# A graph layer's row gathers: 127 partitions on GpSimd, the last partition by SyncE

## The reference

```
h    = max(layernorm(x), 0)                       # 12500 x 64
h0   = attr @ W0 + b0                             # per edge, 32 -> 64
t    = gelu(gelu(h0) @ W1 + b1) @ W2 + b2
score = (h0 + t) @ W3 + b3                        # 412500 x 64
msg  = h[src] * score                             # the gather that the change touches
wV   = segment_sum(msg, dst) / max(count(dst), 1) # 12500 x 64
out  = x + wV @ Wo + bo
```

## Time and profile before

| | |
|---|---|
| median of 3 runs | 4044.81 us |
| span of the profiled execution, first to last instruction | 4042.3 us |
| TensorE busy | 81% of the span |
| GpSimd busy | 75% |
| VectorE, ScalarE busy | 27%, 14% |
| mean granted TensorE clock | 0.785 of full speed |
| mean traffic | 43 GB/s |

### The profile page before, as it was taken

The page is one execution under the profiler, slowest core; times in us unless marked ns, Lnnn a source line. Parts: engine busy times, 40 slices in busy tenths (PEclk is TensorE's granted clock), DMA queues, the critical chain, the costliest instruction groups (busy, mean ns, idle before and its releaser), DMA issues.

```text
span 4042.3 us, 34777 instructions
## 1 busy us (share of the span) xinstructions
PE 3264.8 (81%) x12308; PEld 2146.4 (53%) x12309; DVE 1084.3 (27%) x2563; ACT 585.2 (14%) x838; POOL 3045.3 (75%) x3228
## 2 busy tenths in 40 slices
PE   4988888888888878888888788888887788888879
PEld 2655555555555555555555555555555555555557
DVE  7322222222222222222222222222222222222234
ACT  4211111111111111111111111111111111111111
POOL 7777777777777777777777777777777777777776
PEclk8977777777777777777777777777777777777778
DMA  5211111111111111111111111111111111111112
GB/s 145 48 40 40 40 40 40 40 40 40 40 40 42 40 40 40 40 40 40 40 40 40 40 40 40 40 40 40 41 41 41 40 40 40 40 40 40 40 37 60
DMA packets 217372, 174.70 MB, mean 43 GB/s; under 512 B 112108, under 2 KB 163821, under 8 KB 216920
## 3 DMA queue, kind: packets, MB, share of 16 engines
q0 software_dynamic: 103136, 105.82, 12.1%
q1 hardware_dynamic: 113536, 64.91, 6.0%
q10 hardware_dynamic: 616, 3.20, 0.2%
HBM read 167.28 MB, written 6.40 MB: 43 GB/s over the span
## 4 chain that ended last, share of the span: by engine, by line
POOL 73%; issue 24%; PE 2%; DVE 0%; DMA 0%; POOLq 0%; ACT 0%; DVEq 0%
POOL rows L332 73%; PE ps_h1a L539 0%; PE ps_h1b L539 0%; PE ps_h0a L463 0%; POOLq L353 0%; PE ps_h1b L471 0%; PE ps_h1a L471 0%; PE ps_sb L482 0%; PE ps_sb L477 0%; PE ps_wa L497 0%; PE ps_h0b L463 0%; DMA rows<-h_rows,idx 0%; PE ps_sb L486 0%; PE ps_sa L482 0%; PE ps_sa L477 0%
## 5 line engine op out<-in xcount | busy, mean ns | idle before, releaser
L332 POOL DMA_INDIRECT rows<-h_rows,idx x3175 | 2999.5, 945 | 967.6 <-issue 966.9
L497 PE MATMUL ps_wa<-ln_sq,msg 128*128 128x128 f32 x1616 | 350.1, 385 | 665.6 <-DVE msg L690 665.5
L497 PEld LDWEIGHTS ps_wa<-ln_sq,msg 128*128 128x128 f32 x1616 | 299.2, 276 | 741.2 <-issue 728.1
L690 DVE TENSOR_TENSOR msg<-ps_sa,rows 128x512 f32<-128x512 f32 x202 | 139.7, 691 | 1403.3 <-DMA rows<-h_rows,idx 1391.0
L690 DVE TENSOR_TENSOR msg<-ps_sb,rows 128x512 f32<-128x512 f32 x201 | 139.0, 692 | 1396.8 <-DMA rows<-h_rows,idx 1382.0
L396 ACT ACTIVATE g<-ps_h1a,wp 128x512 f32<-128x512 f32 x202 | 139.0, 688 | 2383.5 <-PE ps_h1a L471 2383.5
L482 PE MATMUL ps_sa<-w_attr,attr 128*128 128x256 f32 x808 | 405.0, 654 | 0.0
L482 PEld LDWEIGHTS ps_sa<-w_attr,attr 128*128 128x128 f32 x808 | 229.8, 314 | 327.0 <-issue 292.6
L477 PE MATMUL ps_sa<-b_last,wp 1*128 1x512 f32 x404 | 403.1, 1097 | 0.0
L486 PEld LDWEIGHTS ps_sa<-w_gelu,g 128*128 128x128 f32 x1616 | 377.5, 321 | 34.3
L486 PE MATMUL ps_sa<-w_gelu,g 128*128 128x128 f32 x1616 | 367.7, 405 | 0.0
(11 more groups left out here) (94 smaller groups left out, 2381.4 us busy)
## 6 DMA issues: line engine op xcount, KB each, us to landing
attr<-in_edges SPq DMA_DIRECT2D x402, 128.0 KB, 3.0
rows<-h_rows,idx POOLq DMA_INDIRECT x3175, 2.4
xs<-in_x SPq DMA_DIRECT2D x4, 700.0 KB
h_rows<-ln_d ACTq DMA_DIRECT2D x4, 700.0 KB
dst_i<-in_dst SPq DMA_DIRECT2D x1, 1612.0 KB, 27.2
idx<-in_src SPq DMA_DIRECT2D x50, 32.0 KB, 2.3
rows<-in_dst_rows SPq DMA_DIRECT2D x4, 384.0 KB
out<-ln_d SPq DMA_DIRECT2D x1, 1530.0 KB
```

Of the source, the lines that this page charges most:

```text
L332: pool.indirect_dma_start(rows[:, slot, t, :], None, table, bass.IndirectOffsetOnAxis(ap=idx[:, part, at, t:t + 1], axis=0),).then_inc(gat ...
L497: pe.matmul(window[0:m * D, 0:m * WIN], msg[:, s % 2, t:t + m, :].rearrange("p t d -> p (t d)"), hot[:, k, t:t + m, :].rearrange("p t n -> ...
L690: dve.tensor_tensor(msg[:, s % 2, 0:n, :], ps_s[s % 2][:, 0:n * D].rearrange("p (t d) -> p t d", d=D), rows[:, s % G_RING, 0:n, :], ALU.mu ...
```

## The change

GpSimd gathers blocks 0 to 15 as before. From block 16 on each gather covers partitions 0 to 126 (NEAR = 127). The row of partition 127 is fetched by SyncE: `edge_rows(b)` waits until the indices are in and the slot is free, loads the 8 row numbers of partition 127 from `idx` into registers and issues 8 copies of one row (256 bytes) each, with the source address made from the register. SyncE does this for block b + 16 ahead of block b's attribute load. VectorE's message waits for a second semaphore, `edge_row_in` of the slot. In the wide program, which does not run with these data, the first 16 blocks are written out so that the slot's first use can be told apart.

```diff
--- before.py
+++ after.py
@@ -49,6 +49,7 @@
 EPS = 1e-5
 
 G_RING = 16
+NEAR = P - 1
 IDX_GROUP = 8
 IDX_GROUPS = 4
 LAG = 8
@@ -180,6 +181,7 @@
         attr_in = [sem(f"attr_in{h}") for h in range(IN_RING // 2)]
         idx_in = [sem(f"idx_in{q}") for q in range(IDX_GROUPS)]
         gathered = [sem(f"gathered{s}") for s in range(G_RING)]
+        edge_row_in = [sem(f"edge_row_in{s}") for s in range(G_RING)]
         h0_done = sem("h0_done")
         g1_done = sem("g1_done")
         h1_done = sem("h1_done")
@@ -284,8 +286,25 @@
                          ).then_inc(base_in, 16)
             sp.dma_start(top[:, :], bounds_dram[1:2, 0:NB]).then_inc(base_in, 16)
 
+            sp.wait_ge(h_out, 32 * LN_STEPS)
+
+            def edge_rows(b):
+
+                slot, group = b % G_RING, b // IDX_GROUP
+                part, at, n = group % IDX_GROUPS, b % IDX_GROUP, tiles_of(b)
+                sp.wait_ge(idx_in[part], uses(group, IDX_GROUPS) * 16)
+                sp.wait_ge(msg_done, b - G_RING + 1)
+                _, nodes = nc.values_load_multi_w_load_instructions(
+                    idx[NEAR:P, part, at, :], engines=(mybir.EngineType.SP,), min_val=0, max_val=N - 1,
+                    skip_runtime_bounds_check_because="a source is a node, and the DMA checks its bounds")
+                for t in range(n):
+                    sp.dma_start(rows[NEAR:P, slot, t, :], h_dram[bass.ds(nodes[t], 1), :]
+                                 ).then_inc(edge_row_in[slot], 16)
+
             def ahead(b, s):
 
+                if b + G_RING < NB:
+                    edge_rows(b + G_RING)
                 if b % 2 == 1 and b + IN_RING - 1 < NB:
                     sp.wait_ge(score_done, b + 1)
                     load_attr(b + IN_RING - 1)
@@ -328,10 +347,11 @@
                 if at == 0:
                     pool.wait_ge(idx_in[part], uses(b, IDX_GROUP * IDX_GROUPS) * 16)
 
+                parts = P if s < G_RING else NEAR
                 for t in range(tiles_of(b)):
                     pool.indirect_dma_start(
-                        rows[:, slot, t, :], None, table,
-                        bass.IndirectOffsetOnAxis(ap=idx[:, part, at, t:t + 1], axis=0),
+                        rows[0:parts, slot, t, :], None, table,
+                        bass.IndirectOffsetOnAxis(ap=idx[0:parts, part, at, t:t + 1], axis=0),
                     ).then_inc(gathered[slot], 16)
 
             for b in range(RAW):
@@ -687,6 +707,8 @@
                 dve.wait_ge(score_done, b + 1)
                 n = tiles_of(b)
                 dve.wait_ge(gathered[s % G_RING], (uses(b, G_RING) - 1) * 16 * TILES + 16 * n)
+                if s >= G_RING:
+                    dve.wait_ge(edge_row_in[s % G_RING], (uses(b, G_RING) - 2) * 16 * TILES + 16 * n)
                 dve.tensor_tensor(msg[:, s % 2, 0:n, :],
                                   ps_s[s % 2][:, 0:n * D].rearrange("p (t d) -> p t d", d=D),
                                   rows[:, s % G_RING, 0:n, :], ALU.mult).then_inc(msg_done, 1)
@@ -879,7 +901,9 @@
                     bias_residual(k, 0)
                 bias_late(0)
                 wide(0, 0)
-                blocks_loop(dve, 1, NB, G_RING, wide)
+                for b in range(1, G_RING):
+                    wide(b, b)
+                blocks_loop(dve, G_RING, NB, G_RING, wide)
                 dve.sem_inc(acc_done, 1)
                 output_early()
 
```

## The result

The changed kernel takes **10517.86 us** (median of 4 runs, 10516.01 to 10521.98) against 4044.72 us for the kernel before in the same comparison: a ratio of 2.600, 95% interval 2.597 to 2.604. The forecast was 4022 us, with a range of 3570 to 4300. It was wrong in sign and in size.

What follows compares the result with a forecast made beforehand. GpSimd's gathers were taken as the bound, with SyncE's copies hidden: 4042.3 - 22.9 = 4019.4 us of span, plus 2.5 us by which the median lies above it, gave 4022 us; range 3570 to 4300.

Steps and rivals of the forecast that it cites:

- What bounds the kernel: GpSimd's gathers set the end at 1.249 us each, 9.99 us a block; TensorE would pass one in 5 to 6.
- 127 is odd: GpSimd's generator with 127 rows, not evenly dealt over 16 engines: at most 31 ns more a gather, taken as 0.
- a sign that I named: Software queue of the gathers: packets per gather fall from 32 if rows go to fewer engines.
- GpSimd does not wait for landings: Gathers on GpSimd: a longer landing counts only once, at the end, 0 to +2.3 us, taken as 0.
- The rule on engines: Gather DMAs: largest number of engines up to 16 dividing the partitions, so 127 on one; 2.3 us if engines take turns.
- slower generation: Rival on GpSimd, 3095 gathers: 127 rows generated another way; at 31 ns 4118 us; chance 0.31, 0.20 of it below 4300.
- Its far ends: Gathers on GpSimd: 945 ns doubled, 6970 us; or all rows on one engine at 2.41 us a gather, about 7640.
- One row less: Each of 3095 gathers on GpSimd saves 7.4 ns, 22.9 us in all; bounds 0 and 30.3 us.
- SyncE's copies: SyncE's loads and 8 copies per block: 5.8 us taken, 6.5 with its other work, hidden in GpSimd's 9.9.
- the low end: SyncE's work per block at its least: one register load and 8 copies, 0.30 + 8 * 0.30 = 2.7 us.
- The new waits: SyncE's wait for the message delays attribute loads, VectorE checks another semaphore: all hidden, nothing new becomes late.
- Landing: End of a gather's transfer: median 2.4 us, longer by about 2.3 us if all rows use one engine.

Runs made afterwards that it cites:

- g112_sp: Changed kernel with 112 in place of 127 partitions in each GpSimd gather from block 16 on, SyncE's copies kept: 3985.46 us, ratio 0.9854 to the kernel before.
- side_tile16: Kernel before, but from block 16 on SyncE copies one whole 128-row gather in each sixteenth block: 4015.0 us, ratio 0.9926.

## Why the prediction was wrong

- **What bounds the kernel: right.** GpSimd set the end before and after, and TensorE's idle time was no cushion. The sum from two terms of one group closes to 4 us.
- **"127 is odd": the step that failed.** I named it the large unknown, and then bounded it on the dear side by SyncE's rows over 96, 4 and 5 partitions: 31 ns, taken as 0. Measured: 1594 ns a gather, 3095 * 1594 = 4933 us, and 1537 us of pauses. Those rows come from another generator and have small counts; none of them had a large prime. That oddness itself was the wrong property is shown by 125. The 32 packets of a gather were read as "8 rows on each of 16 engines", which was right, and the rule that deals them so was then judged by its drain (2.3 us) and not by the entries that GpSimd has to write. That packets per gather would fall from 32 with fewer engines, a sign that I named, was wrong too: they rose to 144.
- **"GpSimd does not wait for landings": failed as well.** It held at 128 partitions. With 127 the transfers come back on GpSimd as the 386 pauses, 1537 us, which shrink with half of the bytes and are gone with the larger ring. What in the transfers it waits for stays open. The engine time of a gather was carried over as 2.43 us; by the queue's share it is 28.8% of 16 * 10520.1 us over 3223 gathers, 15.0 us.
- **The rule on engines.** The trace agrees with the Trainium skill (DMA: Bandwidth & Descriptors, section "Why a DMA increments its semaphore by 16 and not by 1"): the largest number of engines up to 16 that divides the partitions, so 127 rows on one. The bytes above give 1, 5 and 15 engines for 127, 125 and 120. It prices no generation; the runs do.
- **The rival "slower generation": right in place and sign, far too low.** Its far ends, 6970 us for 945 ns doubled and 7640 us for all rows on one engine, came nearest: the dealing of the second was right and its price wrong, since it took the engine's time to drain, 2.41 us, in place of GpSimd's time to write the entries, and neither had the pauses. Most of its chance lay below 4300 all the same, on the 31 ns.
- **One row less: wrong in size.** I took 7.4 ns a row as proportional. On 16 engines 16 rows fewer save 20 or 21 ns, 64 fewer 45 ns: 0.7 to 1.3 ns a row. About 850 ns are fixed (an estimate: 899 less 4 entries by 11 ns). Had 127 been dealt well, the gain would have been a few us (an estimate: 3095 * 0.7 to 1.3 ns is 2 to 4 us).
- **SyncE's copies: right.** Hidden, as g112_sp shows. A block takes one load and 8 * 0.43 us, 4.1 us with the 714 ns of g112_sp, below the 5.8 us taken for it; the low end's one load was right, though it takes 714 ns and not 304. The Trainium skill (DMA: Bandwidth & Descriptors, section "Latency and other measured facts") puts such a load at about 600 ns at least; one of 4 numbers took 557 ns in the median and 458 at the least in side_tile16, so the measurement decides against that floor.
- **The new waits: right as far as shown.** The profiles of g112_sp and of the changed kernel name no wait of TensorE for attributes. VectorE's idle time before its messages is put down to "issue" in g112_sp (1957.9 us), so whether the gather or the row copy came last can't be read there; that the copies cost nothing rests on the time.
- **Landing: the right direction.** 2.4 to 6.2 us in the median, where up to 4.7 was allowed for. The end takes it once; what the transfers cost beyond that is in the pauses.

## What to carry to other kernels

Give GpSimd's gathers a partition count that is a multiple of 16, and when a size is to be shrunk, look at its divisors before its rows: 112 cost 21 ns less than 128, 127 cost 1594 ns more. To take load off a gather engine take whole gathers away, not rows: 49 of 3175 gathers gone, 1.5% of the rows, gave 58.8 us, and half of the rows gone from every gather only 131 us (4044.9 to 3913.9). And where a trace shows an operation at one size only, a bound from another engine's generator is no bound.

## What was not expected of the hardware

- DMA engines that get no row of a gather get as many entries of 4 bytes as the others have rows; the bytes of the queue give their number to within 2 bytes a gather for 127, 126, 125, 120 and 113.
- The 4.2 to 4.5 us pauses ahead of each eighth gather vanish with a ring of 28672 bytes, and their sum grows from 1537 to about 3600 us (4567 - 967) with 8192.
- With gathers this slow TensorE idles more and its granted clock falls, as the stretch from 170 to 1000 us shows (us, PE, PEld, DVE, ACT and POOL busy with counts, clock, DMA share, GB/s), after and before:

```profile
170.00:1000.00 830.00, 329.07 (x963) 212.01 (x961) 77.87 (x191) 43.97 (x64) 632.29 (x250) 0.60 0.31 17
```

```profile
170.00:1000.00 830.00, 674.16 (x2521) 440.17 (x2522) 205.60 (x503) 115.53 (x168) 627.35 (x666) 0.78 0.17 40
```

The mean lies between the levels of 1.2 and 2.4 GHz, and nearer to the lower one than before: 329.07 us for 963 matmuls is 342 ns each, 674.16 for 2521 is 267. It costs nothing here, since TensorE waits for GpSimd.
